# Turning half of k by DMA and making half of M of three fp16 products in a cross-attention and FFN kernel

## What is computed

```python
q, k, v = Wq @ layernorm(x), Wk @ ctx, Wv @ ctx      # 8 heads of 64
q = softmax(q, over the head's 64 channels) / 8
k = softmax(k, over the 1024 tokens)
out = Wo @ ((k @ v.T).T @ q) + bo                    # per head; linear attention
x = x + out / norm(out, over channels) * g * sqrt(128)
x = x + layernorm(x) @ dequant(qweight) + bias       # 1024 by 1024
```

## Time and profile before

| | |
|---|---|
| median of 3 runs | 672.92 us |
| the profiled execution | 670.46 us |
| its span, first to last instruction | 668.7 us |
| granted TensorE clock, mean | 0.987 |
| busy: PE / DVE / POOL / ACT | 95% / 82% / 70% / 68% |

### The profile page before, as it was taken

How to read it: one execution, slowest core, us unless ns; L and a number is a source line. 1 busy time by engine, 2 the same in 40 slices (tenths; PEclk the granted TensorE clock), 3 DMA queues, 4 the chain that set the end, 5 groups by cost and what they waited for, 6 DMA issues and landing times.

```text
span 668.7 us, 10173 instructions
## 1 busy us (share of the span) xinstructions
PE 633.6 (95%) x3285; PEld 385.1 (58%) x3302; DVE 550.3 (82%) x897; ACT 455.1 (68%) x741; POOL 468.5 (70%) x409
## 2 busy tenths in 40 slices
...
DMA packets 179236, 79.35 MB, mean 119 GB/s; under 512 B 168536, under 2 KB 170096, under 8 KB 179184
## 3 DMA queue, kind: packets, MB, share of 16 engines
...
...
## 4 chain that ended last, share of the span: by engine, by line
PE 83%; DVE 6%; ACT 3%; POOL 3%; issue 2%; DMA 1%; another core or an unknown queue 0%; SPq 0%; POOLq 0%; DVEq 0%; ACTq 0%
PE ps_m L1224 14%; PE ps_m L1319 14%; PE ps_k L1154 5%; PE ps_ta L1208 4%; PE ps_k L1155 4%; PE ps_k L1156 4%; PE ps_q L1154 4%; PE ps_q L1156 4%; PE ps_q L1155 4%; PE ps_tb L1208 4%; PE ps_o L1156 4%; PE ps_o L1154 4%; PE ps_o L1155 4%; PE ps_o L1419 4%; PE ps_o L1237 2%
## 5 line engine op out<-in xcount | busy, mean ns | idle before, releaser
L457 POOL TENSOR_TENSOR q_tok_lo<-q_exp,q_tok_hi 128x1024 f16<-128x1024 f32 x64 | 137.7, 2153 | 90.0 <-ACT q_tok_hi L611 88.4
L430 POOL TENSOR_TENSOR q_exp<-q_exp,q_rec 128x1024 f32<-128x1024 f32 x64 | 121.7, 1902 | 5.0
L586 ACT ACTIVATE k_exp<-ps_k,k_nmax 128x1024 f32<-128x1024 f32 x64 | 71.0, 1109 | 76.7 <-DVE k_nmax L858 76.7
L1224 PE MATMUL ps_m<-k_t,c_t 128*128 128x512 f32 x256 | 119.1, 599 | 0.0
L600 ACT ACTIVATE q_exp<-q_exp,w_unit 128x512 f32<-128x512 f32 x128 | 92.0, 720 | 39.0 <-DVE q_exp L870 39.0
L865 DVE TENSOR_REDUCE q_nmax<-ps_q 128x8 f32<-128x512 f32 x128 | 87.7, 685 | 27.6 <-PE ps_q L1156 27.2
L858 DVE TENSOR_REDUCE k_nmax<-ps_k 128x1 f32<-128x1024 f32 x64 | 77.3, 1208 | 19.7 <-PE ps_k L1156 19.7
L870 DVE TENSOR_TENSOR q_exp<-ps_q,q_nmax 128x512 f32<-128x512 f32 x128 | 88.5, 692 | 4.4
L611 ACT ACTIVATE q_tok_hi<-q_exp 128x1024 f16<-128x1024 f32 x64 | 67.5, 1055 | 23.6 <-POOL q_exp L430 23.6
L877 DVE TENSOR_REDUCE q_sum<-q_exp 128x16 f32<-128x1024 f32 x64 | 77.3, 1209 | 0.9 <-ACT q_exp L600 0.8
L1154 PE MATMUL ps_k<-c_hi,wk_lo 128*128 128x512 f32 x128 | 67.5, 527 | 3.3 <-ACT k_exp L586 3.2
...
## 6 DMA issues: line engine op xcount, KB each, us to landing
...
q_hi<-q_tok_hi SPq DMA_TRANSPOSE x64, 3.1
q_lo<-q_tok_lo SPq DMA_TRANSPOSE x64, 3.2
```

The lines of the kernel that those rows point to most:

```text
L430: nc.gpsimd.tensor_tensor(pair, pair, rec.unsqueeze(2).to_broadcast([P, 2 * HEADS, DH]), ALU.mult).then_inc(qs_done, 1)
L457: nc.gpsimd.tensor_tensor(q_tok_lo[p % 2][:], q_exp[:, 2 * p:2 * p + 2, :].rearrange("p t d -> p (t d)"), q_tok_hi[p % 2][:], ALU.subtract ...
L1224: last = nc.tensor.matmul(ps_m[:], c_t[s][:, t, :], k_t[:, t, :], start=(t == 0), stop=(t == TC - 1))
```

## The change

With `TURNED = 2`, chunks 0 and 1 of k are no longer turned on PE. Their exponentials are lifted by 2^12 (ACT adds `ln 2^12` to the negative maximum in one more small instruction, `k_bias`), split into fp16 `k_hi` (ACT, `high_k`) and `k_lo` (POOL, `low_k`), and turned by four more DMA transposes an iteration (`turn_k`). c's scale is now fitted before it is moved (`fit_c` on DVE): `move_tc` writes a scaled fp32 `c_t` and a scaled fp16 `c_t_hi`, and DVE makes `c_t_lo` (`low_tc`). For each token block `mix_m` makes M's left 256 columns of three fp16 matmuls and the right 256 of one fp32 matmul. `split_rs` moves from ACT to POOL, `low_x2` on DVE from step 0 to step 1. `fit_g` becomes `undo_g`, two small instructions in place of five; what depends on `vo` alone is worked out once. For room, some set-up tiles now lie in other tiles (the weights as loaded in `q_exp`, `x2n_hi` and `x2n_lo` in `spare`). Cut to the core:

```diff
 SP, turn_k, and its place
+                for tok, turned, done, turned_sem in ((k_hi, k_t_hi, khi_done, khi_turned),
+                                                      (k_lo, k_t_lo, klo_done, klo_turned)):
+                    sp.wait_ge(done, TURNED * b + j + 1)
+                    if b > 0:
+                        sp.wait_ge(m_ready, b)
+                    sp.dma_start_transpose(turned[:, :, j * P:(j + 1) * P], tok[j][:]).then_inc(turned_sem, 16)
...
                     turn_q(c, 2, "lo")
-                    turn_q(c, 3, "hi")
                 if do_f:
                     sp.wait_ge(x2lo_done, f + 1)
-                    sp.dma_start_transpose(x2_lo[:], x2n_lo[:]).then_inc(x2lo_turned, 16)
+                    sp.dma_start_transpose(x2_lo, x2n_lo).then_inc(x2lo_turned, 16)
                 if do_c:
+                    turn_q(c, 3, "hi")
                     turn_q(c, 3, "lo")
                 if do_a:
+                    for j in range(TURNED):
+                        turn_k(a, j)
                     for p in range(2):
 POOL
+                def low_k(j):
+                    pool.wait_ge(khi_done, TURNED * a + j + 1)
+                    if begun(a):
+                        pool.wait_ge(klo_turned, 16 * TURNED * a)
+                    nc.gpsimd.tensor_tensor(k_lo[j][:], k_exp[:, j, :], k_hi[j][:], ALU.subtract).then_inc(klo_done, 1)
...
                 for j in range(STEPS):
+                    if j == 0 and do_f:
+                        split_rs()
                     if j == 0 and do_c:
                         scale_q(c, 3)
+                    if j == 0 and do_a:
+                        for ch in range(TURNED):
+                            low_k(ch)
                     if j == 0 and do_c:
                         low_q(c, 3)
 ACT
                 def exp_k(b, sums, j):
                     act.wait_ge(kmax_done, 4 * b + j + 1)
-                    if begun(8 * b + 2 * (j - 2) + 2):
-                        act.wait_ge(tk_ready, 8 * b + 2 * (j - 2) + 2)
-                    nc.scalar.activation(k_exp[:, j % 2, :], ps_k[:], ACT.Exp, bias=k_nmax[:, j:j + 1],
+                    bias = k_nmax[:, j:j + 1]
+                    if j < TURNED:
+                        if begun(b):
+                            act.wait_ge(kexp_done, 4 * (b - 1) + j + 1)
+                        nc.scalar.activation(k_bias[:, j:j + 1], bias, ACT.Identity,
+                                             bias=k_lift[:]).then_inc(kbias_done, 1)
+                        act.wait_ge(kbias_done, TURNED * b + j + 1)
+                        bias = k_bias[:, j:j + 1]
+                    held, of = (j - 2, b) if j >= 2 else (j + 2, b - 1)
+                    if of >= 0:
+                        if held < TURNED:
+                            act.wait_ge(klo_done, TURNED * of + held + 1)
+                        else:
+                            act.wait_ge(tk_ready, TK * of + 2 * (held - TURNED) + 2)
+                    nc.scalar.activation(k_exp[:, j % 2, :], ps_k[:], ACT.Exp, bias=bias,
                                          accum_out=k_sum[:, sums, j:j + 1]).then_inc(kexp_done, 1)
...
                     act.wait_ge(tc_ready, 2 * n + h + 1)
+                    act.wait_ge(cfit_steps, 2 * (n + 1))
...
+                    nc.scalar.activation(c_t_hi[1 - s][:, 4 * h:4 * h + 4, :], turned, ACT.Identity,
+                                         scale=c_fit[:]).then_inc(cthi_done, 1)
+                    nc.scalar.activation(c_t[1 - s][:, 4 * h:4 * h + 4, :], turned, ACT.Identity,
+                                         scale=c_fit[:]).then_inc(tc_moved, 1)
...
-                    if 1 <= j < 5 and do_a:
-                        move_tk(2 * (j - 1))
-                    if j in (1, 2) and do_a:
-                        move_tk(2 * (j - 1) + 1)
+                    if TURNED < j < 5 and do_a:
+                        move_tk(2 * (j - 1 - TURNED))
...
                         high_x2()
-                        split_rs(f, rs2)
                     if j == 0 and do_a:
+                        high_k(0)
                         exp_k(a, s, 1)
+                        if TURNED == 2:
+                            high_k(1)
                     if j == 0 and do_c:
                         high_q(c, 3)
 DVE
+                def low_tc(b, sb_, h):
+                    dve.wait_ge(tc_moved, 2 * b + h + 1)
+                    nc.vector.scalar_tensor_tensor(out=c_t_lo[sb_][:, 4 * h:4 * h + 4, :].rearrange("p t c -> p (t c)"),
+                                                   in0=(ps_ta, ps_tb)[h][:], scalar=c_fit[:],
+                                                   in1=c_t_hi[sb_][:, 4 * h:4 * h + 4, :].rearrange("p t c -> p (t c)"),
+                                                   op0=ALU.mult, op1=ALU.subtract).then_inc(ctlo_done, 1)
...
                         if j == 2:
                             sum_q(a, 0)
+                        if j == 1 and do_f:
+                            low_x2(f)
                         max_k(a, j + 1)
-                    if j == 0 and do_f:
-                        low_x2(f)
+                        if j == 2 and TURNED == 2:
+                            low_tc(a, s, 1)
...
                     if j == 5 and do_a:
-                        fit_g()
+                        undo_g()
...
                         top_c()
+                        fit_c()
                     if j == 6 and do_a:
                         sum_q(a, 2)
                     if j == 6 and do_n:
                         norm_x()
+                        low_tc(n, 1 - s, 0)
 PE
                 def transpose_k(k):
-                    pe.wait_ge(kexp_done, 4 * a + k // 2 + 1)
+                    pe.wait_ge(kexp_done, 4 * a + TURNED + k // 2 + 1)
                     if k < 2:
                         pe.wait_ge(tc_moved, 2 * a + k + 1)
+                        pe.wait_ge(ctlo_done, 2 * a + k + 1)
...
                     for t in range(t0, t1):
-                        last = nc.tensor.matmul(ps_m[:], c_t[s][:, t, :], k_t[:, t, :], start=(t == 0),
+                        three(ps_m[:, 0:TURNED * P], c_t_hi[s][:, t, :], c_t_lo[s][:, t, :], k_t_hi[:, t, :],
+                              k_t_lo[:, t, :], start=(t == 0), stop=False)
+                        last = nc.tensor.matmul(ps_m[:, TURNED * P:], c_t[s][:, t, :], k_t[:, t, :], start=False,
                                                 stop=(t == TC - 1))
...
-                    if 1 <= j < 5 and do_a:
-                        transpose_k(2 * (j - 1))
+                    if TURNED < j < 5 and do_a:
+                        transpose_k(2 * (j - 1 - TURNED))
                     if do_a and not (j == 7 and i == END):
                         project_q(j)
-                    if 1 <= j < 5 and do_a:
-                        transpose_k(2 * (j - 1) + 1)
+                    if TURNED < j < 5 and do_a:
+                        transpose_k(2 * (j - 1 - TURNED) + 1)
```

More of the change, by code:

```diff
@@ L109, in build @@
         c_t = [sb(f"c_t{s}", [P, TC, P]) for s in range(2)]
+        c_t_hi = [sb(f"c_t_hi{s}", [P, TC, P], F16) for s in range(2)]
+        c_t_lo = [sb(f"c_t_lo{s}", [P, TC, P], F16) for s in range(2)]
+        c_unit = sb("c_unit", [P, 1])
+        c_fit = sb("c_fit", [P, 1])
+        g_back = sb("g_back", [P, 1])
+        gs_back = sb("gs_back", [P, 1])
         c_abs = sb("c_abs", [P, 1])
@@ L129, in build @@
         k_rec = sb("k_rec", [P, HC])
-        k_t = sb("k_t", [P, TC, HID])
+        k_lift = sb("k_lift", [P, 1])
+        k_bias = sb("k_bias", [P, TURNED])
+        k_hi = [sb(f"k_hi{j}", [P, N], F16) for j in range(TURNED)]
+        k_lo = [sb(f"k_lo{j}", [P, N], F16) for j in range(TURNED)]
+        k_t_hi = sb("k_t_hi", [P, TC, TURNED * P], F16)
+        k_t_lo = sb("k_t_lo", [P, TC, TURNED * P], F16)
+        k_t = sb("k_t", [P, TC, HID - TURNED * P])
         q_tok_hi = [sb(f"q_tok_hi{r}", [P, 2 * HID], F16) for r in range(2)]
@@ L458, in low_q, with split_rs @@
                                             q_tok_hi[p % 2][:], ALU.subtract).then_inc(qlo_done, 1)
+                def low_k(j):
[3 more added lines that the diff above has]
+                    nc.gpsimd.tensor_tensor(k_lo[j][:], k_exp[:, j, :], k_hi[j][:], ALU.subtract).then_inc(klo_done, 1)
+                def split_rs():
+                    pool.wait_ge(x2n_done, f + 1)
+                    if begun(f):
+                        pool.wait_ge(rs_ready, f)
+                    one = ones[:].to_broadcast([P, 3])
+                    nc.gpsimd.tensor_tensor(rs_parts[:, 0:3, 0], rs2[:].to_broadcast([P, 3]), one,
+                                            ALU.mult).then_inc(rs_steps, 1)
+                    pool.wait_ge(rs_steps, 4 * f + 1)
+                    nc.gpsimd.tensor_tensor(rs_rest[:], rs2[:], rs_parts[:, 0, 0:1], ALU.subtract).then_inc(rs_steps, 1)
+                    pool.wait_ge(rs_steps, 4 * f + 2)
```

(20 more changed lines are left out.)

131 lines of the change are left out of this document (83 added, 48 removed).

## The result

Four runs of each kernel on one chip: before 673.02 us (672.76 to 675.30), after **693.04 us** (690.49 to 694.28); the ratio is 1.0285, 95% interval 1.0246 to 1.0324. Slower, as forecast, but by 20.0 us where 10.5 were forecast, and 1 us beyond the range. (The ratios here leave out runs more than 1.5% above the fastest of the same kernel; medians and ranges are of all runs.) The profiled execution took 692.17 us, span 690.3; to a hundredth the spans, 668.67 and 690.35, differ by 21.68.

What follows compares the result with a forecast made beforehand. PE, busy 38.50 of 38.55 us, with a second chain through DVE, ACT and `ps_k` almost as long. 0.84 - 0.42 + 0.32 = +0.74 us, thirteen times, plus 0.84 made +10.5 on 672.92: 683.4 us, range 667 to 692.

Steps and rivals of the forecast that it cites:

- At nothing: Items counted as costing no time: `low_tc(0)`, `fit_c`, ACT's moves, SP's transposes, set-up aliases (plus or minus 1 us).
- PE spared: PE's saved work: 1.74 us of transposes and 0.85 in `mix_m`, together 2.59 us an iteration; a block takes 0.75.
- E to the second transpose: First stretch of the iteration, ending at PE's second transpose: from E + 14.28 to E + 15.12, 0.84 us later.
- E: The end of `exp_k(0)`, from which the forecast counts each iteration; it recurs every 38.55 us before the change.
- two slacks: Places where PE barely avoids waiting before the change: `mix_out(0)` for `g_lo`, 0.30 us; `project_k(2)` for `exp_k(1)`, 0.40 us.
- the port term: `low_x2` on DVE holds the port shared with POOL from E + 7.19 to E + 8.28, delaying `low_k(0)`.
- the last link: `low_tc(1)`, 0.75 us, stands behind `max_k(3)` on DVE; PE's transposes into `ps_tb` wait a microsecond for it.
- To `project_q(7)`, and to E: The other two stretches: PE without a pause, spared 0.42 us; then 7.09 on DVE, with 0.32 added by `k_bias`.
- SP at nothing: Four more DMA transposes on SP cost nothing: each lands 3.2 us after issue, last by E + 23, wanted E + 28.
- `low_k(0)` is in time: Rival: POOL gives `low_k(0)` 0.6 us earlier; iteration +0.13 us, total time 674.7 us; chance 0.25.
- POOL and SP get later still: Third rival: `split_rs` at 1.6 and `k_bias` at 0.45 make an iteration +1.56 us, total time 694 us; chance 0.15.
- PE stays the bound: Rival: all 2.59 us spared on PE is gained each iteration, total time 631.5 us; chance 0.12.

Runs made afterwards that it cites:

- run 1: Changed kernel with POOL's second row-part operation of iteration 0 moved behind both `low_k`: 685.52 us, ratio 1.0235.
- run 5: Changed kernel with POOL's `split_rs` moved from ahead of `scale_q(c,3)` to behind it, still ahead of `low_k(0)`: 689.17 us.
- Run 4: Changed kernel with `low_tc(1)` on DVE moved from behind `max_k(3)` to ahead of `max_k(2)`: 682.81 us, ratio 1.0180.
- run 3: Changed kernel with `k_bias` left out, so chunks 0 and 1 are not lifted by 2^12: 689.79 us.
- run 6: Changed kernel with the edits of run 1 and Run 4 together: 685.83 us, ratio 1.0112.
- run 7: On top of run 6, `high_k(0)` on ACT and `low_k(0)` on POOL come earlier, `high_q(c,3)` behind `exp_k(2)`: 684.92 us, ratio 1.0047.
- run 8: On top of run 7, k's DMA transposes go ahead of q(c,3) on SP, chunk 0's ahead of x2 low: 710.93 us, ratio 1.0566.
- run 9: On top of run 7, k's DMA transposes are spread into gaps of SP's order, k1 low behind q(c,3): 669.33 us, ratio 0.9976.
- run 11: On top of run 6, the SP order of run 9 without the earlier `low_k(0)` of run 7: 682.47 us, ratio 1.0162.

## Why the prediction was wrong

**The step that failed** is that no step of the forecast went through iteration 0. Its only term for the fill is the last of "At nothing": "Set-up aliases touch iterations -1 to 1, where PE isn't the bound throughout: plus or minus 1 us in all, taken as 0". The profiled run is 8.5 later at the first norms, and no run shows that the aliases cost any of it. What the runs show in its place is an order: both `low_k` of iteration 0 stand on POOL behind the row parts, which wait 7.19 for ACT, so `exp_k(2)` waits 2.30 for `low_k(0)` and PE 4.14 for `exp_k(2)`. Undone, it gives back 3 to 7 us, 4.5 by the means of the profiles and 5.0 by the medians (run 1). With 4.5 in the sum the forecast would have been 688. Of the rest of the 21.7, 1.82 lies ahead of the first `exp_k(0)`, with its cause open, 2.7 more than forecast in the first interval and the twelve behind it, and some 2 in the scatter of the fill.

**PE spared**: right. A block takes 0.76 (forecast 0.75). Nothing of it came out as time, as the second chain said.

**E to the second transpose**: right in sum, and within 0.3 at each link. `exp_k(1)` ends at E + 6.77 (6.96), `max_k(2)` starts at E + 8.62 (8.59), `exp_k(2)` at E + 10.16 (10.46), `max_k(3)` at E + 13.13 (13.20), the transposes at E + 15.15 (15.12). Some of that is luck: `exp_k(2)` comes 0.30 early and the way from there to `max_k(3)` is 0.23 longer, and the wait that the forecast put ahead of `project_k(2)`, for `exp_k(1)`, is 0.50 ahead of `mix_out(0)` instead, the other of its two slacks; `project_k(2)`, at 350.42, then starts 0.15 behind the end of `exp_k(1)`. `split_rs` takes 347.30 to 348.28, 0.98 (1.08). Run 5 shows the port term to be a real cost of about 1.03 wherever `low_x2` meets POOL ahead of `low_k(0)`. The Trainium skill (SBUF — State Buffer, SBUF: two separate sides) calls the pair of ports an exclusive lock held for a whole instruction; the rows of run 5, 1.24 in place of 0.20 for three columns, agree. Run 4 shows the last link: with `low_tc(1)` away, 1.03 comes back.

**To `project_q(7)`, and to E**: 16.82 (16.76) and 7.43 (7.41). The sum was +0.74; the usual interval is +0.86.

**One term was on the path by the count only.** E is not the sole start of the circle. The sum holds 0.32 for the `k_bias` ahead of E (the one ahead of `exp_k(1)` is not in it, as `exp_k(2)` waits for `low_k(0)`; the third rival counts 0.16 for it twice all the same). Without both the interval fell by 0.13, because POOL's row has its own way from `attend` over the additions and the statistics to `low_k(0)`, at most 0.21 behind (run 3). The sum held since the two ways are nearly equal.

**SP at nothing**: cost under a microsecond in the changed kernel (two intervals), and held only there. The forecast counted landings of 3.2 behind each issue and did not ask what else is in flight then: already in the changed kernel `c_in` lands after 9.9 in place of 6.2 and `x_in` after 7.8 in place of 5.5, the medians of the two pages. As soon as the iteration is a microsecond shorter, k's last transpose goes out with ACT's three loads, and single iterations lose 3 to 8 us (runs 4, 6, 7), part of it to PE's clock behind the wait. Runs 8, 9 and 11 show that the place of k's transposes on SP decides it; in run 9 the last one goes out 4.8 to 5.0 ahead of the loads. What the transfers contend for is not shown.

**Rivals.** "`low_k(0)` is in time" is out: `exp_k(2)` starts 0.31 behind the end of `max_k(2)` (forecast 0.61). "POOL and SP get later still" had the right time, 694, and the wrong way there: `split_rs` and `k_bias` cost what the forecast said. "PE stays the bound" is out: even in run 9, of 2.59 us spared on PE 0.25 an interval is left (the twelve make 459.49, before 462.55).
